# Sparsemax attention of a long kernel, redone in 16 interleaved units

## What is computed

```python
q, k, v = heads(layernorm(x) @ Wq + bq), heads(ctx @ Wk + bk), heads(ctx @ Wv + bv)
scores = q @ k.T / sqrt(16)              # per batch and head, 512 x 1024
def sparsemax(z):                        # along the keys
    z = z - z.max(-1)
    zs = sort_descending(z);  cssv = cumsum(zs) - 1
    k = number of zs > cssv / rho        # rho = 1, 2, ...
    tau = cssv[k - 1] / k
    return clip(z - tau, 0)
x = x + merge(sparsemax(scores) @ v) @ Wo + bo
```

## Time and profile before

| | |
|---|---|
| runs | 3860.3, 3866.78, 3867.1 us; median 3866.78 |
| profiled execution | 3865.0 us, of which the span on the core is 3863.3; granted clock 0.83 |
| PE | busy 2639.0 us (68%) |
| DVE | 2407.8 (62%) |
| ACT | 1475.5 (38%) |
| POOL | 320.4 (8%) |
| first finished thresholds of l1 / last | 969.4 / 1755.6 us from the span's start |

### The profile page before, as it was taken

One profiled execution on the slowest core, in us unless ns is written; L12 is line 12 of the kernel. 1 busy time (PEld: TensorE's weight loads), 2 busy tenths in 40 slices (PEclk: granted clock), 3 DMA queues, 4 the chain that ended last, 5 costly groups with the idle time before them and its releaser, 6 DMA issues. The chain is left out here.

```text
span 3863.3 us, 39157 instructions
## 1 busy us (share of the span) xinstructions
PE 2639.0 (68%) x11814; PEld 1688.4 (44%) x11814; DVE 2407.8 (62%) x4807; ACT 1475.5 (38%) x2242; POOL 320.4 (8%) x143
## 2 busy tenths in 40 slices
PE   2999996352433322234899995878768598499678
PEld 2444443230111111113788883545433587245367
DVE  4677663848777778873555453665555455587277
ACT  2444441116666766763222212222125122156221
POOL 0000000010000000000222210111110011200021
PEclk8999998575666656666999997889879798789789
DMA  1000000050000000000111101000041110522011
GB/s 56 13 12 13 11 6 35 0 178 6 22 23 23 1 23 22 22 1 32 49 49 49 41 14 41 1 0 0 10 134 42 37 43 17 183 48 67 19 37 35
DMA packets 46338, 136.44 MB, mean 35 GB/s; under 512 B 8568, under 2 KB 18816, under 8 KB 41600
## 3 DMA queue, kind: packets, MB, share of 16 engines
q1 hardware_dynamic: 46208, 135.01, 11.7%
HBM read 106.28 MB, written 28.31 MB: 35 GB/s over the span
## 5 line engine op out<-in xcount | busy, mean ns | idle before, releaser
L1403 ACT ACTIVATE l1a_over_s<-l1a_sc_s,l1a_ntau_s 128x1024 bf16<-128x1024 f32 x272 | 312.2, 1148 | 149.4 <-DVEq L1431 141.4
L1229 PE MATMUL ps<-ident,l1a_worst_s 128*1 128x128 f32 x8 | 3.0, 372 | 484.8 <-DVEq L1490 484.8
L1722 PE MATMUL ps<-m1e_x_part_s,m1e_up_part_s 128*128 128x512 f32 x1296 | 299.1, 392 | 22.0 <-POOL m1e_up_part_s L1818 15.9
L1284 DVE MAX8 l1a_cand_s<-ps 128x8 f32<-128x128 f32 x1024 | 218.4, 284 | 133.2 <-PE ps L1189 127.2
L1722 PEld LDWEIGHTS ps<-m1e_x_part_s,m1e_up_part_s 128*128 128x128 f32 x1296 | 244.5, 189 | 74.5 <-issue 23.7
L1189 PE MATMUL ps<-l1a_ka_s,l1a_qa_s 128*128 128x512 f32 x256 | 146.0, 590 | 110.9 <-ACT l1a_sc_s L1355 90.1
L1355 ACT ACTIVATE l1a_sc_s<-ps 128x512 f32<-128x512 f32 x256 | 153.0, 598 | 168.4 <-DVE l1a_cand_s L1284 168.4
L1229 PEld LDWEIGHTS ps<-ident,l1a_worst_s 128*1 128x1 f32 x8 | 0.6, 79 | 491.6 <-issue 428.7
L1765 ACT ACTIVATE m1e_act_out_s<-ps 128x512 f32<-128x512 f32 x108 | 64.6, 598 | 348.0 <-PE ps L1722 348.0
L973 DVE TENSOR_REDUCE l3a_shift_s<-ps 128x1 f32<-128x1024 f32 x128 | 150.1, 1219 | 65.5 <-PE ps L890 65.5
L543 DVE TENSOR_SCALAR l0a_probs_s<-l0a_probs_s 128x1024 f32<-128x1024 f32 x128 | 88.5, 691 | 150.3 <-ACT l0a_probs_s L610 149.9
(11 more groups left out here) (515 smaller groups left out, 5854.7 us busy)
## 6 DMA issues: line engine op xcount, KB each, us to landing
m1ew_up_s<-m_up SPq DMA_DIRECT2D x9, 1536.0 KB, 6.5
l1a_ka_s<-l_k_parts SPq DMA_DIRECT2D x16, 512.0 KB, 7.8
l3h_ka_s<-l_k_parts SPq DMA_DIRECT2D x16, 512.0 KB, 8.1
m1ew_down_s<-m_down SPq DMA_DIRECT2D x9, 768.0 KB, 4.3
l0a_w_s<-l_w SPq DMA_DIRECT2D x16, 384.0 KB, 3.0
m3ew_up_s<-m_up SPq DMA_DIRECT2D x6, 768.0 KB, 4.2
l_v_groups<-l1p_v_all_s SPq DMA_DIRECT2D x2, 2048.0 KB, 6.6
l1a_qa_s<-l_q_parts SPq DMA_DIRECT2D x16, 256.0 KB, 5.9
```

What stands on the lines that cost most here:

```text
L1284: ins = nc.vector.max(T["cand"][:, r, 8 * (c + j * 4):8 * (c + j * 4) + 8], ps[:, f % 2, c * P:(c + 1) * P])
L1403: nc.scalar.activation(T["over"][:, :], T["sc"][:, r, :], ACT.Relu, bias=T["ntau"][:, r:r + 1], accum_out=T["total"][:, r:r + 1]).then_inc ...
L1722: ins = nc.tensor.matmul(ps[:, 2 * (u % 2) + way, :], up_parts[a][:, k, way, c, :], x_parts[b][:, k, half * BANK:(half + 1) * BANK], start ...
```

## The change

**Attention of l1** is `sparse_attention`, in 16 units: unit u is group u // 2 with half its queries, 8 rows of 128 × 1024. Candidates of unit u + 1, sums of unit u and probabilities of unit u − 1 are interleaved in the order of each engine. The scores are not copied: PE multiplies them a second time (`again`), ACT reads them from PSUM with minus tau as bias, and writes what lies above tau to `sc` while it sums (`first_sums`). Two more passes go over `sc`, on ACT alone (`sums`). The counting pass is gone: the second threshold divides by a count estimated from the candidates, the third by a secant slope. Michelot's iteration has three rounds, and a count behind it. DVE doesn't share in the sums. Denominators are taken at the end, as in `dense_attention`; `slot_sum` falls.

**HeadTiles** serve all three attentions, with v in two buffers instead of three. In the projection the q and k of groups 0 and 1 are loaded after the first half of the units' stores, v is stored in pieces of two of the key tiles, and the third group and v's loads move to the attention's start (`finish_first`). POOL's fills are now in l1's projection too.

```diff
+    def finish_first(self, sp):
+        self.load_qk(sp, 2)
+        for n in range(2):
+            self.load_v(sp, n)
...
-            if tiles is not None:
-                for j in range(3):
-                    sp.wait_ge(hi_stored[j], 16 * len(range(j, U // 2, 3)))
-                    sp.wait_ge(lo_stored[j], 16 * len(range(j, U // 2, 3)))
-                for n in range(tiles.BUFS):
-                    tiles.load_qk(sp, n)
+                if u == U // 2 - 1:
+                    for i in range(3):
+                        sp.wait_ge(hi_stored[i], 16 * len(range(i, U // 4, 3)))
+                        sp.wait_ge(lo_stored[i], 16 * len(range(i, U // 4, 3)))
+                    for n in range(2):
+                        tiles.load_qk(sp, n)
             for b in range(B):
-                sp.wait_ge(v_ready, (b + 1) * TV // B)
-                sp.dma_start(v_groups[4 * b:4 * b + 4].rearrange("g p n -> p g n"),
-                             v_all[:, 4 * b:4 * b + 4, :, :, :].rearrange("p g c h n -> p g (c h n)")
-                             ).then_inc(v_stored, 16)
-            sp.wait_ge(v_stored, 32)
+                for c in range(0, nk // P, 2):
+                    sp.wait_ge(v_ready, b * TV // B + c + 2)
+                    sp.dma_start(v_groups[4 * b:4 * b + 4, :, c * P:(c + 2) * P].rearrange("g p n -> p g n"),
+                                 v_all[:, 4 * b:4 * b + 4, c:c + 2, :, :].rearrange("p g c h n -> p g (c h n)")
+                                 ).then_inc(tiles.v_stored, 16)
...
+            def place(u):
+                buf = u // 2 % BUFS
+                sp.wait_ge(lo_ready, u + 1)
+                if u // 2 >= BUFS and u % 2 == 0:
+                    sp.wait_ge(shift_cleared, u // 2 - BUFS + 1)
+                for tt in range(2):
+                    at = (2 * (u % 2) + tt) * P
+                    for part, src in enumerate((minus_hi, minus_lo)):
+                        sp.dma_start(qa[64 + part:65 + part, buf, :, at:at + P].bitcast(F32),
+                                     src[S * tt:S * tt + S, :].bitcast(F32)).then_inc(shift_placed, 16)
+            tiles.finish_first(sp)
+            for u in range(UNITS):
+                place(u)
+                n = u // 2 - 1
+                if u % 2 == 0 and n >= 0:
+                    sp.wait_ge(pv_done, NC_ * (2 * n + 2))
+                    if n + BUFS < G:
+                        tiles.load_qk(sp, n + BUFS)
+                    if n + 2 < G:
+                        tiles.load_v(sp, n + 2)
...
+            for u in range(UNITS + 1):
+                for r in range(ROWS):
+                    if u < UNITS:
+                        again(u, r)
+                    if r == 1 and u > 0:
+                        turn(u - 1)
+                    if u + 1 < UNITS and 2 <= r < 6:
+                        first_row(u + 1, r - 2)
+                if u == UNITS - 1:
+                    denominators(0)
+                for t in range(NC_):
+                    if u > 0:
+                        second(u - 1, t)
+                    if u + 1 < UNITS and t < 4:
+                        first_row(u + 1, 4 + t)
+                    if u == UNITS and t < PARTS[0][1]:
+                        spread_bank(t)
+                    if u > 0 and t > 0:
+                        value_products(u - 1, t - 1)
+                if u > 0:
+                    value_products(u - 1, NC_ - 1)
...
+            def first_threshold(u):
+                k = u % 2
+                dve.wait_ge(rows_used, FIRST * (u + 1))
+                nc.vector.sem_inc(seen, 1)
+                for r in range(ROWS):
+                    own.done(nc.vector.max(best[:, r, :], cand[:, r, :]))
+                own.done(nc.vector.reduce_max(last[:, :], cand[:, :, :].rearrange("p r (c e) -> p r c e", e=8)[:, :, :, 7],
+                                              AX.X))
+                own.wait()
+                for j in range(1, 8):
+                    own.link(nc.vector.tensor_tensor(best[:, :, j], best[:, :, j], best[:, :, j - 1], ALU.add))
+                own.link(nc.vector.scalar_tensor_tensor(best[:, :, :], best[:, :, :], -1.0,
+                                                        ranks[:, :].unsqueeze(1).to_broadcast([P, ROWS, 8]),
+                                                        ALU.add, ALU.mult))
+                own.link(nc.vector.reduce_max(tau[:, k, :], best[:, :, :], AX.X))
+                for i in range(MICHELOT + 1):
+                    own.link(nc.vector.tensor_tensor(above[:, :, :], cand[:, :, :], wide(tau[:, k, :], CAND), ALU.is_gt))
+                    own.link(nc.vector.reduce_sum(number[:, k, :], above[:, :, :], AX.X))
+                    if i < MICHELOT:
+                        own.done(nc.vector.tensor_tensor(above[:, :, :], above[:, :, :], cand[:, :, :], ALU.mult))
+                        own.link(nc.vector.reciprocal(rcount[:, :], number[:, k, :]))
+                        own.link(nc.vector.reduce_sum(slope[:, :], above[:, :, :], AX.X))
+                        own.link(nc.vector.scalar_tensor_tensor(tau[:, k, :], slope[:, :], -1.0, rcount[:, :],
+                                                                ALU.add, ALU.mult))
+                nc.vector.tensor_scalar(minus_tau[:, k, :], tau[:, k, :], -1.0, None, ALU.mult).then_inc(tau_set, 1)
+                own.link(nc.vector.tensor_tensor(last[:, :], last[:, :], tau[:, k, :], ALU.subtract))
+                own.link(nc.vector.tensor_scalar(last[:, :], last[:, :], 0.5, 5e-7, ALU.mult, ALU.max))
+                own.link(nc.vector.reciprocal(rgap[:, k, :], last[:, :]))
...
+            def second_threshold(u):
+                k = u % 2
+                dve.wait_ge(pair_used, again_place(u, ROWS - 1) + 1)
+                own.link(nc.vector.tensor_scalar(excess[:, 0, :], total[:, 0, :], -1.0, None, ALU.add))
+                own.link(nc.vector.scalar_tensor_tensor(slope[:, :], excess[:, 0, :], 0.0, rgap[:, k, :],
+                                                        ALU.max, ALU.mult))
+                own.link(nc.vector.scalar_tensor_tensor(slope[:, :], slope[:, :], float(nk - CAND), number[:, k, :],
+                                                        ALU.min, ALU.add))
+                own.link(nc.vector.reciprocal(rcount[:, :], slope[:, :]))
+                own.link(nc.vector.tensor_tensor(step[:, :], excess[:, 0, :], rcount[:, :], ALU.mult))
+                nc.vector.tensor_scalar(minus_step[:, :], step[:, :], -1.0, None, ALU.mult).then_inc(step_set, 1)
...
+            def settle(u):
+                k = u % 2
+                dve.wait_ge(summed, 2 * ROWS * u + 2 * ROWS)
+                own.link(nc.vector.tensor_scalar(excess[:, 2, :], total[:, 2, :], -1.0, None, ALU.add))
+                own.done(nc.vector.tensor_reduce(worst[:, :], excess[:, 2, :], AX.X, ALU.max, apply_absolute_value=True))
+                own.link(nc.vector.tensor_tensor(excess[:, 2, :], excess[:, 2, :], rstep[:, :], ALU.mult))
+                nc.vector.sem_inc(worst_ready, 1)
...
+            for u in range(UNITS):
+                if u > 0:
+                    cut(u - 1)
+                if u + 1 < UNITS:
+                    for r in range(ROWS // 2):
+                        candidates(u + 1, r)
+                second_threshold(u)
+                if u + 1 < UNITS:
+                    for r in range(ROWS // 2, ROWS):
+                        candidates(u + 1, r)
+                third_threshold(u)
+                if u + 1 < UNITS:
+                    first_threshold(u + 1)
                 else:
-                    nc.vector.reduce_max(shift[:, :], half_max[:, :, :], AX.X).then_inc(shift_ready, 1)
-
-            def cut(n):
-
-                dve.wait_ge(shift_turned, n + 1)
-                if not (isinstance(n, int) and n == 0):
-                    dve.wait_ge(shift_placed, 32 * n)
-                nc.vector.tensor_scalar(minus_hi[:, :], ps[0:ROWS, 7, 0:P], -1.0, None, ALU.mult).then_inc(hi_ready, 1)
-                dve.wait_ge(hi_ready, n + 1)
-                nc.vector.scalar_tensor_tensor(minus_lo[:, :], ps[0:ROWS, 7, 0:P], -1.0, minus_hi[:, :].bitcast(F32),
-                                               ALU.mult, ALU.subtract).then_inc(lo_ready, 1)
-
-            def finish(n):
-                dve.wait_ge(o_summed, n + 1)
-                nc.vector.reciprocal(rden[:, :], ps[:, 7, :]).then_inc(rden_ready, 1)
-                dve.wait_ge(rden_ready, n + 1)
-                nc.vector.tensor_tensor(o_all[:, bass.ds(n, 1), :].rearrange("p a n -> p (a n)"), o_raw[:, :],
-                                        rden[:, :], ALU.mult).then_inc(o_done, 1)
-
-            def first():
-                if sparse:
-                    for j in range(8):
-                        nc.vector.memset(T["ranks"][:, j:j + 1], 1.0 / (j + 1)).then_inc(ones_set, 1)
-                    nc.vector.memset(T["zero"][:, :], 0.0).then_inc(ones_set, 1)
-                    dve.wait_ge(ones_set, 9)
-
-
```

(53 more changed lines are left out.)

636 lines of the change are left out of this document (268 added, 368 removed).

## The result

The changed kernel takes 3722.3 us (median of 4 runs, 3717.6 to 3727.0) against 3865.1 of the kernel before; the ratio is 0.9632, with a 95% interval of 0.9616 to 0.9649. It is 143 us faster where 3714 and −152.6 were forecast. Its profiled execution has a span of 3725.1 us (before 3863.3).

The account below looks back on a forecast made before the run. It took a ring through DVE and ACT in l1's sparse attention, 45.0 us a unit in six steps, as the bound; −137.3 (l1) −6.5 −8.5 −0.3 = −152.6 us gave 3714 on the median, range 3670 to 3768.

Parts of the forecast that it names:

- Rival A: The forecast as worked out: 3714 us, with 43.5 to 46.8 us a unit giving about 3692 to 3741; chance 0.59.
- Steps 2, 4 and 5: Loop of l1: second threshold 2.3 us, third threshold 2.1, next unit's first threshold 15.4 with no slack on DVE or ACT.
- Step 3: Loop of l1, sums 1 on ACT: 8 × 1.27 = 10.2 us, with DVE's second half of candidates fitting beside it.
- Step 6: Loop of l1, settle: 3.1 us as before plus 0.3 for other products in PE's queue, 3.4.
- Unit 15: Last unit of l1's loop: estimated 42.6 us, no next threshold, but twelve denominator products (5.6), sums 2 and bare settle.
- Step 1: Loop of l1, eight first sums from PSUM on ACT, with PE's mixed queue: 11.6 us, bounds 9.8 and 12.2.
- Fill: Start of l1: projection lengthened, attention at 873.7, first candidates 874.9, eight rows to 890.1, first threshold to 905.2.
- Drain: End of l1: turn to first probability 6.1 us, eight steps at 1.13 and 0.5, products 1.8, denominators to scaling 9.6.
- Other stages: Attention of l3 starts earlier, −6.5 us; m2 likewise, −8.5; two v buffers nothing; constant −0.3.
- B: Loop of l1: PE never late and wakes hide in each other, 42.5 us a unit, 3677 us; chance 0.18.
- D: Check at settle's end fails, DVE runs its 20 exact rounds, some 400 us per such unit, 4114 us; chance 0.04.
- E: No overlap: DVE and ACT wait for each other as before, 56 us a unit, about 3866 to 3875; chance 0.04.

Follow-up runs that it names:

- experiment 2: Changed kernel with four rounds of Michelot's iteration (3750.2 us, ratio 0.9696), or with two and a looser check bound (3704.9 us, 0.9586).
- experiment 1: Changed kernel, but each ACT sum over sc waits for the sum before it instead of the one before that: 3738.7 us, ratio 0.9674.
- experiment 3: Changed kernel with settle cut in two, its first four operations after two rounds, PE turning the worst ahead of value products 4: 3674.7 us, ratio 0.9499.
- experiment 4: Changed kernel with two instead of four rows of next first scores between PE's second scores, six behind: 3749.3 us, ratio 0.9713.
- experiment 7: Changed kernel with settle cut, late loads and fills, last count behind the shift's cut; sums 2 in halves 3652.4 us (0.9449), in one piece 3657.2 (0.9459).

## Why the prediction was right, and where it was not

- **The bound.** That a ring through DVE and ACT sets the pace and not the load of either: right. Over the 15 periods, 669 us, DVE is busy 454 and ACT 531. Rival A came true. Of the loads themselves DVE's was too high: 41 a unit, measured 454/15 = 30, mainly as eight maxima in a row are busy 1.68, so 0.21 each where the sum took 0.284. Nothing in the forecast hung on it.
- **Steps 2, 4 and 5.** Counted from rows of single operations, right to 0.6 us. In step 5 the forecast had both engines end together. DVE is done at 15.0 but the end is set by ACT and PE, whose pairs of second products and value products take 2.2 us a piece at the low clock (experiment 2). So the sign given for this step, ACT idle under 1.5 us beside it, did not hold: it waited 1.42 and 1.14 for PE.
- **Step 3, mis-sized:** 10.2, measured 9.15. The row showed 1.27 between two sums, and the code of the kernel before makes each wait for the one before; the new code does not. I carried a pitch over without asking what set it (experiment 1).
- **Step 6, mis-sized:** 0.3 us for "other products in PE's queue", measured 1.85 of waiting. The queue at that moment should have been written out: products 6 and 7 wait for ACT's last probabilities, then come four second scores at the low clock. Unit 15 has the same error and larger: forecast 42.6 with a settle of 3.4, measured 46.8, as DVE is ready early there and waits 6.81 for the turn behind the last value products (1606.59 to 1613.89 for the last four probabilities, their products and the turn).
- **Step 1.** 11.6, measured 12.0. The forecast's two ends were 10.7 with the clock high and 12.2 with it low throughout; the loop takes 10.6 where it is granted 1.00 and 12.0 at 0.72 (experiment 3), so the size of the clock's part was right. Two of PE's four mixed rows cost some 1.2 of it (experiment 4). The granted clock in the four quarters of the unit shown was 0.72, 0.84, 0.70 and 0.66, neither of its levels throughout, so a value between was the right choice. That an idle array falls to half rate is what the Trainium skill says ("TensorE: Matmul & The Clock Gate", "What's actually happening"). The last quarter agrees, as PE had been idle 6.92 us before it; that step 1 runs at 0.72 or at 1.00 behind the same pause of 1.9 us is not explained by it.
- **Its bounds.** The low ends add up to 42.2 and the high ones to 46.5, not to 42.3 and 46.8; 44.58 lies within either.
- **Fill.** Attention began at 874.4 (forecast 873.7), first maxima 875.5 (874.9), tau at 905.1 (905.2). The working held, but the sign offered for it ("roundings in 25 us") forgot the wait for stores that the same paragraph had worked out: they took 40.
- **Drain, mis-sized.** From the last settled threshold to the output projection it was 35.9 us, forecast 27.0. Two rows of the timeline of PE:

```profile
1620.89 1.22 PE L1175 MATMUL ps<-l1h_qa_s,l1h_ka_s 128*128 128x256 f32 x4 [4.22 <-DMA l1h_qa_s<-l1a_minus_lo_s]
1622.05 0.79 PE L1216 MATMUL ps<-l1a_rden_parts_s,spread 64*128 64x512 f32 x1
...
1624.64 1.08 PE L1187 MATMUL ps<-l1a_probs_s,l1h_v_s 128*32 128x256 f32 x8
```

  A step there is second products, a spread bank and value products, 2.9 us on PE, where I took ACT's 1.13. The spread products weren't counted at all, and where the clock is high second products and value products take 0.73 and 0.64 us in the loop. The loop, 6 us ahead of the forecast up to there (2 from the fill and unit 0 and 8 from units 1 to 14, less 4 in unit 15), hid most of the error, which is luck again: l1 was forecast at −137.3 and came to −133.6.
- **Other stages.** Forecast −8.5 for m2 and −6.5 for l3; −3.1 and −3.0 in the profile, −4.2 and −5.6 over six. In l3 the attention did start earlier, but by 4.8 rather than 6.5: v is done 62.9 us after the block's start instead of 60. And 1.9 of it were given back in the first group: the turns of the shift of groups 0 and 1 are 25.7 apart instead of 23.8, as the third group's and v's loads now stand ahead of the first shift on SP's queue. In m2 the gain was half of what I took: −2.0 to −3.1 in the profiles where one rounding stands 6.63 us, −5.2 to −6.3 in those without. Of the 10 us between forecast and result some 4 are l1's and some 5 these two.
- **The rivals.** B needed PE never late, C its order as the bound; what was measured lies between, nearer A. B counted 20 us of products on PE in a period; it was busy 27.8 of the 44.7 us of the unit shown. D did not occur, and E is excluded by the period.

## What to carry over

When a loop is rebuilt as a ring through several engines, write out for each wait not only the operation that ends it but the whole in-order queue in front of that operation at that moment; the errors in settle, in unit 15 and in the drain, and the experiments that backfired, were queues. A start-to-start pitch read from a trace is the price of an operation with its waits: look at the code's semaphores before carrying it over. And an engine's idle slot in such a ring may be what keeps another's queue moving.

## Not expected of the hardware

- A sum of 128x1024 on ACT starts 1.13 us after the last when two are in flight, 1.27 when each waits for the other; reading its accumulator (0.19 us) overlaps.
- The same step of the same loop, behind the same pause of PE of 1.9 us, was granted 0.72 of the clock in most units and 1.00 in a few, and took 12.0 or 10.6 us. With the pause down to at most 0.7 us it was 1.00 in 11 of 14 units, without one in experiment 7 it was 0.63 to 1.00.
- A rounding on DVE that meets fills on POOL may stand for more than one of them, and not in every run of the same code: 6.63 us in m2, where a fill takes 1.80 to 2.08, in three of six profiles, and at most 1.75 in the others.

```profile
2668.21 6.63 DVE L779 CAST m2p_hi_s<-m2p_full_s 128x512 fp32r<-128x512 f32 x1
```

- Reading a flag into a register and the branch take 1.46 us on DVE, a third of settle.
